# Second attention: where the transpositions of the weights stand in TensorE's order

## The reference, cut to what matters

```python
qkv = x @ Wqkv.T + bqkv
scores = einsum('bhnd,bhond->bhno', q, K_all) * scale + pos_bias   # K_all: keys at the 38 distances
scores = where(n_idx[:, None] < offs[None, :], -inf, scores)
alpha = softmax(scores, axis=-1)
out = einsum('bhno,bhond->bhnd', alpha, V_all)
return (flat * sigmoid(x @ Wgate.T + bgate)) @ Wout.T + bout
```

## Time and profile before

| | |
|---|---|
| median of 3 runs | 1504.06 us (1499.51 to 1507.79) |
| profiled execution | 1515.03 us, span in the profile 1513.2 us |
| mean granted TensorE clock | 0.893 of full |
| second attention, scores of tile 0 to the last tiles | about 987 to 1297 us of the span |
| busy over the span | PE 1247.5 us (82%), DVE 1114.4 (74%), ACT 815.7 (54%), POOL 685.6 (45%) |
| chain that ended last, by engine | PE 43%, DVE 28%, POOL 9%, ACT 8%, issue 6% |
| the two score turns, L1659 | 4096 products in 32 tiles |
| the transpositions, L1676 | 256, 8 for each tile; 29 steps (t = 3 to 31) hold both them and scores |

### The profile page before, as it was taken

One profiled execution on the slowest core, in us unless ns is written; L12 is line 12 of the kernel. 1 busy time (PEld: TensorE's weight loads), 2 busy tenths in 40 slices (PEclk: granted clock), 3 DMA queues, 4 the chain that ended last, 5 costly groups with the idle time before them and its releaser, 6 DMA issues.

```text
span 1513.2 us, 40070 instructions
## 1 busy us (share of the span) xinstructions
PE 1247.5 (82%) x14676; PEld 892.7 (59%) x14676; DVE 1114.4 (74%) x3616; ACT 815.7 (54%) x1971; POOL 685.6 (45%) x1042
## 2 busy tenths in 40 slices
PE   4499889988899988999988899589989998647780
PEld 2255545555455554555556899467777777547660
DVE  5588687886878868888665665558788878755666
ACT  1155555555555555555555455178787657326663
POOL 3023241233432334323223654466666768674664
PEclk9699999999999999999999899777887757668995
DMA  5656727556275572755741311022111112222335
GB/s 120 108 96 91 115 29 117 87 92 107 30 121 81 91 115 28 119 81 91 119 181 35 102 47 30 25 69 63 46 45 44 35 34 76 99 68 81 89 85 173
DMA packets 73892, 123.37 MB, mean 82 GB/s; under 512 B 17534, under 2 KB 46083, under 8 KB 72800
## 3 DMA queue, kind: packets, MB, share of 16 engines
q1 hardware_dynamic: 63896, 104.97, 36.6%
q0 software_dynamic: 7616, 13.59, 2.8%
q10 hardware_dynamic: 2184, 2.25, 0.8%
HBM read 30.40 MB, written 17.60 MB: 32 GB/s over the span
## 4 chain that ended last, share of the span: by engine, by line
PE 43%; DVE 28%; POOL 9%; ACT 8%; issue 6%; DMA 3%; ACTq 1%; DVEq 1%; SPq 0%; POOLq 0%
DVE first L843 7%; PE A L640 6%; DVE S L846 4%; PE S L1099 4%; PE S L611 4%; PE S L622 4%; PE S L1659 3%; DVE tA L822 3%; POOL xq L1468 2%; PE A L1670 2%; PE A L1106 2%; DMA Qp<-mT 2%; DVE tB L823 2%; PE S L1645 2%; PE S L1676 2%
## 5 line engine op out<-in xcount | busy, mean ns | idle before, releaser
L727 ACT ACTIVATE P<-S 128x512 f32<-128x512 f32 (+3 forms) x768 | 330.6, 491 | 285.6 <-PE S L622 283.3
L622 PE MATMUL S<-Qp,Kp 121*128 121x512 f32 (+3 forms) x768 | 258.2, 394 | 39.1 <-DMA Qp<-mT 11.8
L907 POOL TENSOR_SCALAR_AFFINE_SELECT P<-P 128x256 f32<-128x256 f32 x256 | 112.6, 443 | 373.8 <-ACT P L727 373.1
L846 DVE CUSTOM_DVE_ANT_0 S<-S,later 128x512 f32<-128x512 f32 (+3 forms) x512 | 238.9, 514 | 53.7 <-PE S L611 52.4
L611 PE MATMUL S<-Kp,Qp 120*128 120x512 f32 (+3 forms) x768 | 243.4, 389 | 30.7 <-DMA Kp<-big 16.3
L622 PEld LDWEIGHTS S<-Qp,Kp 121*128 121x128 f32 x768 | 137.4, 190 | 123.9 <-DVE first L843 24.6
L843 DVE TENSOR_REDUCE first<-S 128x1 f32<-128x512 f32 x256 | 164.3, 682 | 55.0 <-PE S L611 54.5
L611 PEld LDWEIGHTS S<-Kp,Qp 120*128 120x128 f32 x768 | 132.9, 194 | 112.5 <-issue 49.7
L640 PE MATMUL A<-P,V 128*9 128x256 f32 (+1 forms) x2816 | 174.5, 343 | 5.4 <-POOL P L907 4.6
L640 PEld LDWEIGHTS A<-P,V 128*9 128x9 f32 x2816 | 63.9, 90 | 70.9 <-issue 29.8
L1896 POOL TENSOR_TENSOR prod<-mid,kT 128x128 f32<-128x128 f32 x160 | 68.0, 459 | 72.1 <-ACT mid L1727 45.4
(11 more groups left out here) (358 smaller groups left out, 2585.7 us busy)
## 6 DMA issues: line engine op xcount, KB each, us to landing
Qp<-big SPq DMA_DIRECT2D x63, 256.0 KB
Kp<-big SPq DMA_DIRECT2D x62, 256.0 KB
Qp<-big SPq DMA_DIRECT2D x63, 128.0 KB
Kp<-big SPq DMA_DIRECT2D x62, 128.0 KB
xq<-xq SPq DMA_DIRECT2D x71, 72.0 KB
yb<-yq SPq DMA_DIRECT2D x8, 528.0 KB, 7.2
big<-in_w SPq DMA_DIRECT2D x4, 1024.0 KB, 9.9
big<-vt SPq DMA_DIRECT2D x32, 128.0 KB
```

Of the source, the lines that this page charges most:

```text
L622: te.matmul(S[s][:, 512 * h + c:512 * h + 512], K[0:121, h, 128 * kb:128 * kb + 128], Q[0:121, h, 512 * qh + c:512 * qh + 512], start=True ...
L727: se.activation(k.P[(w.n - 1) % NP0][:, h, c:512], S[s][:, 512 * h + c:512 * h + 512], ACT.Exp, scale=SCALE0).then_inc(p.done("st").h, 1)
L846: ins = ve.tensor_tensor_reduce(out=of, in0=of, in1=k.later[:, 512 - n:512], scale=1.0, scalar=-3e38, op0=ALU.add, op1=ALU.max, accum_out= ...
L907: ge.affine_select(P[:, :, c:c + 128], P[:, :, c:c + 128], [[0, 2], [1, 128]], ALU.is_ge, 0.0, base=0, channel_multiplier=-1).then_inc(p.s ...
```

## The change

The scores become two items. `sc0`, turn 0, is put in the list ahead of `pt`; `sc`, turn 1, stays where both turns were. TensorE's step is then `av`, `sc0`, `pt`, `sc`, `lo`. The waits for keys, masked queries and for DVE's read of the scores before move with turn 0 ahead of `pt`; the wait for the end of turn 0 stands ahead of turn 1, now behind `pt`. The products themselves, their operands and their number stay, and no other engine's order changes. A function `keep_awake` is added; nothing calls it.

```diff
@@ order
             if t >= 4:
                 self.slot["av", t - 4] = o.add("av", t - 4, ring="V").slot
+            if t < NT:
+                o.add("sc0", t)
             if 0 <= t - 3 < NT:
                 o.add("pt", t - 3, ring="P")
@@ attn1_tensor
-        elif w.kind == "sc":
+        elif w.kind in ("sc0", "sc"):
             t = w.at[0]
-            c, i = t // 4, t % 4
-            pe.wait_ge(p.done("k1"), 2 * c + 2)
-            pe.wait_ge(p.sem("a_qm"), 2 * c + 2)
-            for turn in range(2):
-                for j in range(4):
...
-                if turn == 0:
-                    pe.wait_ge(p.sem("pe_sc0"), 2 * w.n)
-            ins.then_inc(p.made("sc").h, 1)
+            c, i, turn = t // 4, t % 4, int(w.kind == "sc")
+            if turn == 0:
+                pe.wait_ge(p.done("k1"), 2 * c + 2)
+                pe.wait_ge(p.sem("a_qm"), 2 * c + 2)
+                if t:
+                    pe.wait_ge(p.done("sc"), t)
+            else:
+                pe.wait_ge(p.sem("pe_sc0"), 2 * w.n)
+            for j in range(4):
...
+            if turn:
+                ins.then_inc(p.made("sc").h, 1)
```

More of the change, by code:

```diff
@@ L1611, in attn1_sync, with keep_awake @@
         ye.dma_start(two.small[n][:], p.a[n]).then_inc(p.sem("d_f1").h, 16)
+def keep_awake(te, p, bank):
+    bits = p.ident[:].bitcast(BF16)
+    te.matmul(bank, bits[:, 0:128], bits[:, None, :].broadcast_to([128, 2, 256]), start=True, stop=True)
 def attn1_tensor(p, k, one, pe, te):
@@ L1647, in attn1_tensor @@
             ins.then_inc(p.made("vw").h, 1)
-        elif w.kind == "sc":
+        elif w.kind in ("sc0", "sc"):
             t = w.at[0]
-            c, i = t // 4, t % 4
-            pe.wait_ge(p.done("k1"), 2 * c + 2)
-            pe.wait_ge(p.sem("a_qm"), 2 * c + 2)
-            for turn in range(2):
-                for j in range(4):
[L1655 to L1662, removed]
-                if turn == 0:
-                    pe.wait_ge(p.sem("pe_sc0"), 2 * w.n)
-            ins.then_inc(p.made("sc").h, 1)
+            c, i, turn = t // 4, t % 4, int(w.kind == "sc")
[7 more added lines that the diff above has]
+            for j in range(4):
+                for g in (turn, 2 + turn):
+                    rows, h = slice(32 * g, 32 * g + 32), 4 * g + j
+                    for q in range(4):
+                        at = WAY - 32 + 128 * i + 32 * q
+                        ins = te.matmul(C[32 * q:32 * q + 32, 64 * h:64 * h + 64], k.Qm[c % 2][rows, j, 128 * i + 32 * q:128 * i + 32 * q + 32],
+                                        k.kT[c % 2][rows, at:at + 64], start=True, stop=True, tile_position=(32 * g, 32 * q))
+                    if turn == 0 and j == 3:
+                        ins.then_inc(p.sem("pe_sc0").h, 1)
+            if turn:
+                ins.then_inc(p.made("sc").h, 1)
         elif w.kind == "lo":
```

## The result

The changed kernel takes 1534.99 us (median of 5 runs, 1526.93 to 1538.45) where the kernel before, beside it, takes 1499.51 (5 runs, 1497.72 to 1507.79): a ratio of 1.0194, 95% interval 1.0157 to 1.0232. It is slower by some 29 us. (The two medians lie 35 us apart, because these five runs of the kernel before are on the quick side. Against the mean of its 105 other runs on record, 1505.3 us, the changed kernel's mean of 1534.2 us is a ratio of 1.019.) The direction was forecast; the size, 9 us, was not, and 1535 lies outside the range.

A forecast was written before the change was run, and what follows sets the result against it. TensorE was taken to bound most tiles, busy 282.43 of the stage's 310 us. Lateness costs of 13.4 us, less 2.7 swallowed and 1.5 gained, made it 9.2 us slower: 1513 us, range 1496 to 1524.

The forecast's parts named there:

- What it removes: Idle weight loads between the two score turns, 0.25 us a tile: at most 7.3 us go, 1.5 us taken as gain.
- (a): Third tile of a chunk: keys come 0.85 us later where TensorE waits for them, 3 tiles, 2.6 us.
- (b): Fourth tile of a chunk: ScalarE runs without a gap to the last masked queries, which end 0.85 us later.
- (c): Chunk starts: transpositions, free before, follow the wait for masked queries, 1.02 us; with late queries 1.87 us at five starts, 9.4 us.
- delays nothing further: Chunks 1 and 2: ScalarE's copy comes about 2 us later, but its exponentials waited for VectorE anyway (2.15 us).
- What swallows part of it: Unexplained idle stretches within the scores, 8.8 us: a later TensorE waits less in them, 2.7 us taken as credit.
- In a tile where ScalarE only waits for TensorE, this costs nothing: the wait moves.: Transpositions and ScalarE's copy begin one turn later, 0.83 us at full clock; free wherever ScalarE is only waiting.
- the gain from the drains: Idle time saved between TensorE's score turns: 0 to 0.25 us a tile, 0.05 taken, 1.5 us in all.
- Even: Idle time between turns goes whole (7.3 us), late queries cost only at five plain chunk starts; 1505 us, chance 0.20.
- Not slower, by the clock: Transpositions between turns break the runs behind which TensorE's clock falls to half, 8 us gained; 1496 us, chance 0.22.
- Slower still, by the clock: Longer waits at chunk starts put transpositions at half clock, 6.2 us, and three stretches stay at half, 4.5 us; 1524 us, chance 0.13.

## Why the forecast had the direction and not the size

**What it removes: right, and too small.** The waits between the turns fell from 32 to 3, as said, and the gain is 0.15 us in the one tile compared, by estimate 4 us in all, where 1.5 was taken and 7.3 allowed. The Trainium skill, "TensorEngine Tiling (Array Packing)", section "Key Properties", has a change of tiling mode drain the engine. In this trace the step from `av` (128x32 tiles) to turn 0 (32x32 tiles) shows no idle time, and that into turn 1 from whole-array transpositions shows 0.17 us: the rule holds here for the second alone. It doesn't bear on the loss, as this term was a gain.

**(a), third tiles: a cost is there, by another way.** It is 5 us alone (1.5 to 9), which holds the 2.6 of the forecast. But the wait for the keys, from which the 2.6 was made, did not grow in that run (1.0 us), and with the new order everywhere it is 2.0 and 4.0 us for 2.1 and 2.5.

**(b) and (c), fourth and first tiles: right in size.** 5 us for the one and 7.7 for the other, 13 in all, each uncertain by some 4 to 5 us, against 9.4 + 1.7 + 0.65 - 0.9 = 10.9 in the forecast. The waits for the queries grew to 13.9 us, "12 or more" having been named as the sign. Two terms in them were taken too small: the transpositions behind the queries ran at half clock at three of seven chunk starts (1.97 us at chunk 2, where 1.02 was taken), and the lateness in the fourth tiles is 1.65 us, not 0.85. Part of that lateness is the wait for VectorE's read of the old scores, for which the forecast took nothing and at worst 1.02 us once or twice: it is 2.25 us in tile 31. That ScalarE's copy, late by some 2 us at chunks 1 and 2, "delays nothing further" was nearly so at chunk 2: of 2.86 us, 0.59 reached the exponentials.

**What swallows part of it: not borne out.** 2.7 us of the unexplained idle time were to vanish. It was 8.8 and 14.2 us in the two profiles of before and 10.0 and 7.7 in those after (all rows), so executions differ by more than the term, and a credit was booked that no run shows. What the timelines do show is that such a stall, formerly behind the transpositions, now stands ahead of them in turn 0, on ScalarE's path.

**The step that failed: "In a tile where ScalarE only waits for TensorE, this costs nothing: the wait moves."** The 44.4 us of ScalarE's waits were read as room, and lateness as one turn, 0.85 us (some 2 us at two chunk starts), that counts only in the places (a) to (c). And the sum has no term for TensorE's clock, which stands in the rivals alone.

Shown: an item that is put ahead of another brings its waits along. The transpositions are 2.74 us late in the first tiles, where turn 0 waits for the queries, and 1.65 us in the fourth. Made late by 0.9 us without such waits, in every tile, they cost some 5 us (1.0000 against 0.9966, intervals that meet).

Shown too: the loss goes through ScalarE. With 37 us less work on it the loss falls from 29 to 5 us, though the waits for the queries stay. So ScalarE's waits were not room to spare. TensorE's waits for ScalarE grew by 16.5 and 18.5 us in the two pairs of profiles; the queries have 6.5 and 7.3 of these, and the copy of the values and the routing, which the forecast left out, 8.4 and 5.5. The reading that fits is that ScalarE's waits are what brings it back into step after a late start.

On record as well: the changed kernel's timed runs have a clock lower by 0.015, which by the estimate above goes with some 12 us. With ScalarE's work cut the clock is back at 0.899, so it too hangs on ScalarE's load. Whether the longer waits lower it, or by what else, no run shows.

Only just shown, by the gap of 0.80 ± 0.71%: the sum of the places is less than the whole. Argued from it, and not shown, is that with the old order in the neighbouring tiles a delay of ScalarE is made good in the next tile, and with the new order in all of them it is carried on to the copies and the gate for which TensorE now waits in L194, L1707 and L1358. No run followed one delay from tile to tile.

In numbers: 13.4 us before credits in the forecast, 11.9 with the gain from the drains; 17 to 19 us by the places measured alone, that gain in it, uncertain by some 10; 29 us together, of which 11 to 18 are idle time of TensorE in the stage.

**The rivals.** "Even" is out by the interval. "Not slower, by the clock" is out too: the order was slower, and the clock of the timed runs fell. The Trainium skill's rule against it ("TensorE: Matmul & The Clock Gate", section "Part 4: PE-mode transpose") was not put to the test. The forecast held against that rule, but these rows don't tell what transpositions do by themselves: ahead of the transpositions at 1059.61 TensorE had worked without a gap, on products of several kinds, from 1051.18 us on. "Slower still, by the clock" gave 1524 us, nearest to the result, and is in part borne out: its first half, transpositions at half clock at the chunk starts, came at three of seven, by its own price 3 x 0.88 = 2.6 us for 6.2, and the lower clock of the timed runs is of its kind. It isn't the whole: at nearly equal clock, 0.89 and 0.90 in the stage, there is still a loss, 1.014, and the split order with less work on ScalarE runs at the clock of before.

**What stays open.** The clock's share of the 29 us: 8 us by the loss at raised clock (21 us, with a wide interval), 12 by the clocks of the timed runs. Why the clock is lower. And the cause of the unexplained idle time in the scores.

## What to carry to other kernels

Before moving an item on an engine that works in order, list the waits of what is put ahead of it, not only its duration: the moved item inherits them. An engine that waits in most tiles is not free for that: count how long its queue runs without a gap up to the next thing that somebody waits for, and whether each tile's waits are what makes up for the last one's delay. Book no credit for idle time whose cause isn't known. And compare the clock over all timed runs before saying from two profiles that a change has none.

## What the runs showed of the hardware

- Four dense products a tile added nothing to the time (1.0005): the granted clock in the stage was 0.89 with them, 0.75 and 0.79 without, and TensorE's busy time 261 us with them, 263 and 271 without. By line (busy us, mean ns of one) the added products are:

```profile
L1617 PE MATMUL S<-ident 128*128 128x512 bf16 x61 | 25.1, 411 | 6.6 <-ACT Qm L1744 5.4 <-DVE sc L1833 1.2
L1617 PE MATMUL A<-ident 128*128 128x512 bf16 x60 | 24.8, 413 | 0.3 <-DVE at L1857 0.3
```

  Their times overlap those of their neighbours, so the 50 us of the two rows are an upper bound of what they add. The rows of all other products add up to 249 us in this stage, for 291 and 283 without.

- The granted clock was 0.61 with the transpositions behind both turns, 0.75 and 0.79 with them ahead of both: the same instructions took 311 us for 263 and 271.
- Two executions of one kernel differ by 9 to 11 us in TensorE's busy time in this stage (271.39 and 262.87; 265.37 and 276.25). A loss of 1% is not to be read from one pair of profiles.
- Over 105 executions of the kernel before, the granted clock of the whole launch lay between 0.884 and 0.910, and on a straight line through them a clock lower by 0.01 goes with a time longer by 8 us.
